# Joining the blocks of the first edge layer, doubling the gather rings, and making the transposed one-hot matrix on ScalarE

## The chip, the cores and the metric

The kernel runs on one core of one Trainium2 chip. The metric is the device time of one execution in microseconds; lower is better. Shares and clocks below are those of the hardware profiler for one profiled execution.

## The reference

Two graph layers follow each other on N = 12,500 nodes with 128 features and E = 212,500 edges (100,000 random edges in both directions and one loop for each node), sorted by destination.

```python
edge_index = jnp.stack([src, dst])
x = _layernorm(x + L0(x, edge_attr_128, WQ, WK, WV, WE, ..., edge_index), axis=-1)
x = _layernorm(x + L1(x, edge_index, W, att_src, att_dst, ..., W1, ..., W2, ...), axis=-1)

# L0: attention over edges, 8 heads of 16
Q, K, V = x @ WQ, x @ WK, x @ WV ;  Eh = edge_attr @ WE
score = K[src] * Q[dst] / sqrt(16) * Eh
score = exp(clip(score.sum(-1), -5, 5))
wV = segment_sum(V[src] * score, dst) ;  Z = segment_sum(score, dst)
h = x + wV / (Z + 1e-6) ;  return batch_norm(h)

# L1: graph attention, softmax over the edges of a destination
xl = x @ W ;  e = leaky_relu((xl @ att_src)[src] + (xl @ att_dst)[dst], 0.2)
alpha = exp(e - segment_max(e, dst)[dst]) / segment_sum(...)
out = segment_sum(alpha * xl[src], dst) + bias
h = bn_relu(out @ W1 + b1) ; h = bn_relu(h @ W2 + b2) ; return h + x
```

All arithmetic is float32.

## The kernel before

Nodes are padded to NP = 12,800 and worked in NG = 25 groups of 512. Edges are worked in NC = 416 chunks of 512, K = 4 slots of 128 edges, one edge per partition. As edges are sorted by destination, the destinations of a chunk nearly always lie in a window of W = 64 nodes that begins at the chunk's first destination (`base_row` holds these bases; the chunks that reach further are worked over again in the `far_windows` functions). Each function is a block of its own: its engines run free of each other, tied by semaphores, and meet at its end.

`prologue` makes the bases and `dst_local`, destination minus base, from the index tables. `project` works the node groups: TensorE transposes x (L341), ScalarE copies it out (L366), TensorE multiplies by the three weight matrices at once (L355), ScalarE evicts Q (L377), VectorE evicts K and V (L391) and copies the transposed x to the third plane of `acc` (L386); SyncE stores `q_table` and `kv_table` in DRAM. `acc` is the accumulator in SBUF, 128 partitions by three planes of 12,800.

`edges0` runs the chunks of the first layer. `U` = 4 is the depth of its rings of data, `V` = 8 that of its index ring and, in layer 1, of its data rings. For each chunk:

- SyncE loads `idx` (L428), the transposed edge features `eat` (L431, 256 KB) and the 64 rows `qw` of `q_table` (L435). These loads, for the chunk four ahead, wait for `spread` of this chunk.
- GpSimd issues four indirect gathers of 128 rows of `kv_table` (L460) into ring slot c mod 4, once TensorE has counted `summed` for the chunk four before.
- VectorE makes `hot` (L548), the 512x64 one-hot matrix, from `dst_local` and `iota`, both in SBUF, three chunks ahead.
- TensorE runs, in this order, the four transposes of `hot` of chunk c+2 into PSUM (`turn`, L479), then for chunk c+1 four matmuls of edge features by WE (L488) and four that spread the Q rows over the edges with the transposed one-hot matrix (L491), which count `spread`, then for chunk c the sums over the window, values (L498) and weights (L500), which count `summed`. The sums wait for VectorE's `valued`.
- ScalarE copies the transposed one-hot matrix out of PSUM for chunk c+2 (L524), then exponentiates the scores of chunk c+1 (L531).
- VectorE multiplies keys by queries (L559), by edge features (L562), reduces over heads (L564), clips (L567), adds the sums of chunk c to `acc` (L581), and weighs the values in place (L573).

`nodes0` divides by the denominators, which go out to DRAM and come back in another layout before they are inverted (L923) and broadcast, adds x on GpSimd (L817), normalizes, and projects for layer 1. `edges1` runs the chunks again with a running maximum: four gathers of 66-float rows on GpSimd (L1064, ring of 8, waiting for `summed`), logits on ScalarE (L1129), mask and maximum on VectorE (L1154 compares with `iota` in SBUF, L1163, L1167), two small transposing products on TensorE (L1081, L1085), `newm` and the shift on VectorE (L1182, L1189), exponentials and the copy of the maximum back to `acc` on ScalarE (L1119 to L1121), then the sums (L1092, L1093) and their addition to `acc` (L1208). `nodes1` finishes.

`alone` is a pass through a semaphore that separates instructions with two waits; `landed` works out the count that a semaphore has when a slot's transfer is in; `over_chunks` runs a body over all chunks in a hardware loop unrolled by its last argument.

Of the kernel before, what the change touches and what calls it, by code (L numbers as in the profile page):

```python
# [21 lines left out]
P = 128  # L22
D = 128
# [10 lines left out]
U, V = 4, 8  # L34
# [12 lines left out]
PIECES = ((0, 3), (3, 12), (12, NG))  # L47
LEAD = 2
# [5 lines left out]
assert V % U == 0 and NG * SG == N and (NG - 5) % 4 == 0 and CR * CJ == NC and LAST % K == 0 and NG % 2 == 1  # L54
# [113 lines left out]
def build(nc, x, src, dst_rows, dst_cols, edges, weights, vectors, out):  # L168
    with ExitStack() as ctx:
# [18 lines left out]
        m["far_table"] = dram("far_table", [NC], I32)  # L188

        m["acc"] = sb("acc", [P, 3, NP])  # L190
# [11 lines left out]
        prologue(nc, m, dst_rows, dst_cols, weights, vectors)  # L202
        project(nc, m, x)
        edges0(nc, m, src, edges)
        far_windows0(nc, m, src, edges)
        nodes0(nc, m)
        edges1(nc, m, src)
        far_windows1(nc, m, src)
# [3 lines left out]
def prologue(nc, m, dst_rows, dst_cols, weights, vectors):  # L212

    with ExitStack() as ctx:
        sem = lambda name: counted(nc, ctx, m, name)
        sb = lambda name, shape, dt=F32: ctx.enter_context(nc.sbuf_tensor(name, shape, dt))
        weights_in, rows_in, cols_in = sem("weights_in"), sem("rows_in"), sem("cols_in")
        base_ready, base_stored, base_back = sem("base_ready"), sem("base_stored"), sem("base_back")
        ident_zero, made, step = sem("ident_zero"), sem("made"), sem("pro_step")

        rows = m["acc"][0:CR, 0, 0:CJ * CE].rearrange("p (j e) -> p j e", e=CE)
        low = m["acc"][0:CR, 1, 0:CJ * CE].rearrange("p (j e) -> p j e", e=CE)
        rows_i = m["acc"][0:CR, 2, 0:CJ * CE].bitcast(I32).rearrange("p (j e) -> p j e", e=CE)
        cols_i = m["acc"][:, 0, CJ * CE:CJ * CE + NC * K].bitcast(I32).rearrange("p (c k) -> p c k", k=K)
# [6 lines left out]
        far_row = sb("far_row", [P, NC + 1])  # L231
        block = ctx.enter_context(nc.Block())

        @block.sync
        def _(sp):
            sp.dma_start(rows_i, dst_rows.rearrange("(p j) e -> p j e", j=CJ)).then_inc(rows_in, 16)
            sp.dma_start(cols_i, dst_cols).then_inc(cols_in, 16)
            sp.wait_ge(base_ready, 1)
            sp.dma_start(m["base_table"].rearrange("(p j) -> p j", j=CJ), base_i[0:CR, :]).then_inc(base_stored, 16)
            sp.dma_start(m["far_table"].rearrange("(p j) -> p j", j=CJ), far_i[0:CR, :]).then_inc(base_stored, 16)  # L240

            sp.wait_ge(base_stored, 32)
# [5 lines left out]
        @block.scalar  # L248
        def _(act):
            act.dma_start(m["w"][:], weights).then_inc(weights_in, 16)  # L250
            act.dma_start(m["vec"][:], vectors).then_inc(weights_in, 16)
            act.wait_ge(weights_in, 32)

        @block.gpsimd
        def _(pool):
# [8 lines left out]
            nc.gpsimd.memset(m["power"][:], -0.5).then_inc(made, 1)  # L264
            pool.wait_ge(made, 4)

        @block.vector
        def _(dve):
# [11 lines left out]
            nc.vector.tensor_copy(far_i[0:CR, :], far_f[0:CR, :]).then_inc(base_ready, 1)  # L280
            dve.wait_ge(cols_in, 16)
            do(nc.vector.tensor_copy(m["dst_local"][:], cols_i))
            dve.wait_ge(base_back, 48)
# [6 lines left out]
            do(nc.vector.tensor_copy(m["base_row"][FAR_ROW:FAR_ROW + 1, NC:NC + 1], reach[:, NC:NC + 1]))  # L290


def project(nc, m, x):

    with ExitStack() as ctx:
        sem = lambda name: counted(nc, ctx, m, name)
        sb = lambda name, shape, dt=F32: ctx.enter_context(nc.sbuf_tensor(name, shape, dt))
        ps = lambda name, shape: ctx.enter_context(nc.psum_tensor(name, shape, F32))
        x_in = [sem(f"x_in{s}") for s in range(4)]
        stored = [sem(f"qkv_stored{s}") for s in range(2)]  # L300
        turned, copied, kept = sem("x_turned"), sem("xt_copied"), sem("xt_kept")
        projected, q_out, kv_out = sem("projected"), sem("q_out"), sem("kv_out")
        xn = sb("xn", [P, 4, T, D])
        xt = sb("xt", [P, 2, G])
        q = sb("q", [P, 2, T, D])
        kv = sb("kv", [P, 2, T, 2 * D])
        ps_xt = ps("ps_xt", [P, 2, G])
        ps_qkv = ps("ps_qkv", [P, T, G])
        xg = x.rearrange("(g k p) d -> g p k d", k=T, p=P)
        qg = m["q_table"].rearrange("(g k p) d -> g p k d", k=T, p=P)  # L310
        kvg = m["kv_table"].rearrange("(g k p) d -> g p k d", k=T, p=P)
        wqkv = m["w"][:, WQ:WV + 1, :].rearrange("p a d -> p (a d)")
        block = ctx.enter_context(nc.Block())

        @block.sync
        def _(sp):
            lead(sp, [*stored], DMA_LEAD)
            for s in range(4):
                sp.dma_start(xn[:, s], xg[s]).then_inc(x_in[s], 16)

            def body(g, s):
                if exists(g + 4):
                    sp.wait_ge(turned, g + 1)
                    sp.dma_start(xn[:, s], row(xg, g + 4)).then_inc(x_in[s], 16)
# [9 lines left out]
        def _(pe):  # L334
            lead(pe, [projected], LEAD)
            def turn_x(g, s):
                pe.wait_ge(x_in[s], landed(g, s, 16, 4))
                if not (isinstance(g, int) and g < 2):
                    pe.wait_ge(kept, g - 1 + LEAD)
# [1286 lines left out]
```

## Time and profile before

| | before |
|---|---|
| runs | 5929.43, 5932.58, 5944.88 us, median 5932.58 |
| profiled execution | 5944.3 us, of it span 5942.5 |
| TensorE busy | 4076.5 us, 69% of the span |
| VectorE busy | 3282.2 us, 55% |
| GpSimd busy | 3368.5 us, 57% |
| ScalarE busy | 1399.3 us, 24% |
| first and last gather of layer 0 | 121.6 and 2886 us |
| first and last gather of layer 1 | 3180.5 and 5706.5 us |

The profile is of one execution; the engine rows give the time in which instructions were recorded as running. A matmul's end is modelled in it. "Idle before" is the time in which an engine stood before an instruction, with what it waited for: "remote" means a semaphore that another engine raised later than the recorded end of its instruction, "issue" that nothing in the profile shows a wait. The granted clock of TensorE is given in shares of full speed.

### The profile page before, as it was taken

What the parts mean: (1) busy time and instruction counts of PE and PEld (TensorE: products, weight loads), DVE (VectorE), ACT (ScalarE), POOL (GpSimd) and SP (SyncE); (2) the same over time, 40 slices, a digit from 0 to 9 for tenths busy, and PEclk for the clock granted to TensorE, in tenths of its full rate; (3) what the DMA queues carried; (4) which work ended last, traced back from release to release, by engine and by line L of the source; (5) the groups of instructions that cost most, each with busy time, mean ns of one, the idle gap of its engine ahead of it and who ended that gap; (6) DMA issues with size and microseconds to landing.
All of it is one profiled execution on the core that took longest, in us unless ns stands there. A gap on an engine that the chain in (4) does not pass through costs nothing. (4 is left out here: it accounts for less than half of the span.)

```text
span 5942.5 us, 93441 instructions
## 1 busy us (share of the span) xinstructions
PE 4076.5 (69%) x21439; PEld 3506.1 (59%) x21440; DVE 3282.2 (55%) x8432; ACT 1399.3 (24%) x4197; POOL 3368.5 (57%) x3417
## 2 busy tenths in 40 slices
PE   5888888888888888888455555555555555555553
PEld 3777787887777777777423444444444444444431
DVE  5554555555555555555474555555555555555555
ACT  2111111111111111111043222222222222222224
POOL 1565555565556555656334666666666666666621
PEclk8787877777778777878676555555555555555566
DMA  7444444444444444444522222222222222222223
GB/s 215 119 126 121 125 123 122 124 125 124 123 123 128 121 123 124 127 121 130 99 58 70 50 51 49 51 50 50 50 51 50 50 51 49 50 51 50 51 69 85
DMA packets 482022, 538.82 MB, mean 91 GB/s; under 512 B 250299, under 2 KB 341053, under 8 KB 481366
## 3 DMA queue, kind: packets, MB, share of 16 engines
q0 software_dynamic: 133120, 330.78, 21.5%
q1 hardware_dynamic: 348199, 203.99, 14.1%
q10 hardware_dynamic: 672, 3.74, 0.5%
q14 instruction: 23, 0.19, 0.0%
q8 instruction: 8, 0.13, 0.0%
HBM read 497.64 MB, written 40.50 MB: 91 GB/s over the span
## 5 line engine op out<-in xcount | busy, mean ns | idle before, releaser
L460 POOL DMA_INDIRECT kv_g<-kv_table,idx x1664 | 1642.8, 987 | 1242.4 <-issue 442.2
L1064 POOL DMA_INDIRECT xg<-xl_table,idx x1664 | 1629.5, 979 | 917.4 <-issue 473.2
L1092 PE MATMUL ps_sum<-pw,xg 128*128 128x64 f32 x3328 | 819.2, 428 | 523.9 <-DVE pws L1194 380.3
L1092 PEld LDWEIGHTS ps_sum<-pw,xg 128*128 128x128 f32 x3328 | 741.0, 328 | 645.9 <-DVE pws L1194 469.4
L498 PE MATMUL ps_sum<-hot,kv_g 128*128 128x64 f32 x3328 | 566.2, 325 | 267.7 <-issue 134.7
L559 DVE TENSOR_TENSOR prod<-ps_q,kv_g 128x512 f32<-128x512 f32 x416 | 286.7, 689 | 803.5 <-remote 526.8
L531 ACT ACTIVATE pex<-score 128x512 f32<-128x512 f32 x416 | 261.6, 629 | 1883.5 <-DVE score L567 1328.6
L498 PEld LDWEIGHTS ps_sum<-hot,kv_g 128*128 128x128 f32 x3328 | 502.4, 231 | 342.9 <-issue 162.2
L488 PE MATMUL ps_eh<-w,eat 128*128 128x128 f32 x3328 | 598.2, 331 | 48.5 <-issue 46.4
L491 PE MATMUL ps_q<-qw,hott 64*128 64x128 f32 x3328 | 578.1, 317 | 42.2 <-issue 40.9
L488 PEld LDWEIGHTS ps_eh<-w,eat 128*128 128x128 f32 x3328 | 548.7, 245 | 70.5 <-issue 64.7
L500 PE MATMUL ps_sum<-hot,pex 128*128 128x64 f32 x3328 | 558.9, 322 | 11.1 <-issue 10.7
L491 PEld LDWEIGHTS ps_q<-qw,hott 64*128 64x128 f32 x3328 | 480.9, 217 | 115.3 <-issue 82.8
L1119 ACT COPY acc<-newm 128x64 f32 x416 | 102.0, 245 | 1831.1 <-remote 1145.0
L500 PEld LDWEIGHTS ps_sum<-hot,pex 128*128 128x128 f32 x3328 | 521.5, 238 | 8.2 <-issue 7.5
L1081 PE MATMUL ps_top<-ident,top 128*64 128x128 f32 x416 | 163.8, 394 | 416.4 <-DVE top L1167 215.0
L1129 ACT ACTIVATE lg<-adw,xg 128x64 f32<-128x64 f32 x1664 | 436.3, 332 | 26.4 <-issue 23.4
L1085 PE MATMUL ps_max<-ident,col 64*128 64x64 f32 x832 | 285.4, 445 | 194.7 <-issue 185.7
L581 DVE TENSOR_TENSOR acc<-acc,ps_sum 128x128 f32 x416 | 120.3, 289 | 475.5 <-PE ps_sum L500 190.2
L479 PE MATMUL ps_hott<-ident,hot 128*64 128x128 f32 x1664 | 323.9, 325 | 60.3 <-DVE hot L548 32.7
L1085 PEld LDWEIGHTS ps_max<-ident,col 64*128 64x128 f32 x832 | 207.5, 309 | 249.4 <-issue 199.8
L1208 DVE TENSOR_TENSOR acc<-acc,ps_sum 128x128 f32 x416 | 117.4, 282 | 428.7 <-remote 406.9
(138 smaller groups left out, 5201.3 us busy)
## 6 DMA issues: line engine op xcount, KB each, us to landing
eat<-in_edges SPq DMA_DIRECT2D x416, 256.0 KB
kv_g<-kv_table,idx POOLq DMA_INDIRECT x1664
xg<-xl_table,idx POOLq DMA_INDIRECT x1664
idx<-in_src SPq DMA_DIRECT2D x832, 2.0 KB
qw<-q_table SPq DMA_DIRECT2D x416, 32.0 KB
adw<-ad_row SPq DMA_DIRECT2D x416, 32.0 KB
kv_table<-kv SPq DMA_DIRECT2D x25, 512.0 KB, 4.1
xl_table<-xl SPq DMA_DIRECT2D x25, 264.0 KB
```

The lines of the kernel that those rows point to most:

```text
L460: nc.gpsimd.indirect_dma_start(out=kv[:, u, k], out_offset=None, in_=m["kv_table"], in_offset=bass.IndirectOffsetOnAxis(ap=idx[:, i, k:k + ...
L479: mm = nc.tensor.transpose(ps_hott[0:W, u % 2, at(k, P)], hot[:, u, k], m["ident"][:])
L488: nc.tensor.matmul(ps_eh[:, b, k], eat[:, u, at(k, P)], m["w"][:, WE], start=True, stop=True)
L491: mm = nc.tensor.matmul(ps_q[:, b, k], hott[:, b, at(k, P)], qw[:, u], start=True, stop=True)
L498: nc.tensor.matmul(ps_sum[:, b, 0:W], kv[:, u, k, D:2 * D], hot[:, u, k], start=(k == 0), stop=(k == K - 1))
L500: mm = nc.tensor.matmul(ps_sum[:, b, W:2 * W], pex[:, b, k], hot[:, u, k], start=(k == 0), stop=(k == K - 1))
L531: nc.scalar.activation(pex[:, b].rearrange("p k (h d) -> p (k h) d", d=DH), score[:, b].unsqueeze(2).to_broadcast([P, K * H, DH]), ACT.Exp ...
L559: nc.vector.tensor_tensor(prod[:].rearrange("p (k d) -> p k d", d=D), ps_q[:, b], kv[:, u, :, 0:D], ALU.mult).then_inc(mult, 1)
L1064: nc.gpsimd.indirect_dma_start(out=xg[:, u, k], out_offset=None, in_=m["xl_table"], in_offset=bass.IndirectOffsetOnAxis(ap=idx[:, u, k:k + ...
L1085: nc.tensor.matmul(ps_max[:, u % 2, 0:W], col[:, u % 2:u % 2 + 1].to_broadcast([W, P]), m["ident"][0:W, 0:W], start=True, stop=True).then_ ...
L1092: nc.tensor.matmul(ps_sum[:, b, 0:W], xg[:, u, k, 0:D], pw[:, b, k], start=(k == 0), stop=(k == K - 1))
L1129: last = nc.scalar.activation(lg[:, u % 4, k], adw[:, u], ACT.Identity, bias=xg[:, u, k, D:D + 1])
```

## The change

The prologue, the projection and the edge stage of layer 0 become one block. x is no longer transposed on TensorE: the host passes `xk`, x transposed with the columns of each group reordered, and `xt`, x transposed. All keys and values are projected first (25 groups of four 128x256 matmuls), evicted by ScalarE alone, and stored in rows of 4 KB, then all queries. GpSimd's gathers start when the keys and values are stored, beside the projection of the queries. Edges of a chunk lie as slot by partition, and the indices of eight chunks are loaded at once.

`acc` has two planes; the third is allocated behind the edge stage and loaded from `xt` in `nodes0`, in the queue behind the store of the denominators and ahead of the load that brings them back. GpSimd's addition of x waits for it.

In the edge stage the ring of gathered rows goes from 4 to 8 in layer 0 and from 8 to 16 in layer 1; the other rings keep depth 4 (layer 0) or 8 (layer 1). TensorE's `turn` is gone, and so is the pass through a semaphore in it. In its place a new DRAM table holds destination minus base for each edge; SyncE loads the chunk's 512 values broadcast over 64 partitions (`local`, 128 KB), and ScalarE makes `hott` = relu(1 - |local - p|) in two steps. `iota` is read from PSUM in the comparisons of both layers. The loops are unrolled twice as far on most engines, one memset moves from VectorE to GpSimd, the last chunk makes one gather instead of four, and in layer 1 the masked logits and `fade` lie in PSUM.

```diff
-U, V = 4, 8
+U, V = 8, 16
+B = 8
+STAGES = 3
-        m["acc"] = sb("acc", [P, 3, NP])
+        m["local_table"] = dram("local_table", [NC, CE])
+
+        m["acc"] = sb("acc", [P, 2, NP])
...
+            def load_local(c, u):
+                sp.dma_start(local[:, u % 4], m["local_table"][bass.ds(c, 1), :].partition_broadcast(W)).then_inc(local_in[u % 4], 16)
...
+            def body(c, v, peeled):
+                sp.wait_ge(spread, c + 1 + LEAD)
+                if not (peeled and c + 4 >= NC):
+                    load_local(c + 4, v)
+                    load_edges(c + 4, v)
+                    load_window(c + 4, v)
+                if v % B == 5 and not (peeled and c + 11 >= NC):
+                    sp.wait_ge(kv_in[7], landed(c, v % U, 16 * K, U))
+                    load_src((c - v) * K + (v // B + 2) * (B * K), v // B)
...
+            for s in range(STAGES):
+                pool.wait_ge(kv_stored[s], 16 * (-(-(NG - s) // STAGES)))
+            for u in range(U):
+                gather(u, u)
...
+            for g in range(NG):
...
+                for k in range(T):
+                    mm = nc.tensor.matmul(ps_pair[:, g % 2, k // 2, at(k % 2, 2 * D)], nodes_x[:, g, k], wkv, start=True, stop=True)
...
+            def copy_out(c, u, first=False):
+                b = u % 2
+                act.wait_ge(local_in[u % 4], landed(c, u % 4, 16, 4))
+                if not first:
+                    act.wait_ge(spread, c - 1 + LEAD)
+                nc.scalar.activation(hott[:, b], local[:, u % 4], ACT.Abs, bias=line[0:W]).then_inc(apart, 1)
+                act.wait_ge(apart, c + 1)
+                nc.scalar.activation(hott[:, b], hott[:, b], ACT.Relu, bias=1.0, scale=-1.0).then_inc(copied, 1)
...
-            def turn(c, u):
-                pe.wait_ge(hot_ready, c + 1)
-                pe.wait_ge(copied, c - 1 + LEAD)
-                alone(pe, m["passed"])
-                for k in range(K):
-                    mm = nc.tensor.transpose(ps_hott[0:W, u % 2, at(k, P)], hot[:, u, k], m["ident"][:])
-                mm.then_inc(turned, 1)
...
-                                        m["iota"][:].unsqueeze(1).to_broadcast([P, K, W]),
+                                        ps_iota.unsqueeze(1).to_broadcast([P, K, W]),
                                         ALU.is_equal).then_inc(hot_ready, 1)
...
             sp.dma_start(m["den_rows"], acc[0:P:DH, 1, :]).then_inc(den_out, 16)
+            for piece, (first, end) in enumerate(PIECES):
+                sp.dma_start(third[:, first * G:end * G], xt[:, first * G:end * G]).then_inc(xt_in[piece], 16)
             sp.wait_ge(den_out, 16)
             sp.dma_start(den[:], m["den_rows"].rearrange("h (a n) -> (h a) n", a=P // H)).then_inc(den_in, 16)
...
-        xg = sb("xg", [P, V, K, ROW1])
-        lg = sb("lg", [P, 4, K, W])
+        raw = sb("raw", [P, 4, K, W])
+        ps_lg = ps("ps_lg", [P, 4, G])
+        lg, fade = ps_lg[:, :, 0:K * W].rearrange("p b (k w) -> p b k w", w=W), ps_lg[:, :, K * W:(K + 1) * W]
```

## Rows read from the trace of the kernel before

**Rows 1.** The page: span, busy time and share of each engine, instructions.

```profile
span 5942.5 us, 93441 instructions
PE 4076.5 (69%) x21439; PEld 3506.1 (59%) x21440; DVE 3282.2 (55%) x8432; ACT 1399.3 (24%) x4197; POOL 3368.5 (57%) x3417
```

**Rows 2.** Stages: length, PE, PEld, DVE, ACT, POOL busy (count), clock, DMA, GB/s.

```profile
0.00:120.00 120.00, 81.04 (x300) 49.26 (x301) 63.48 (x90) 35.44 (x77) 1.14 (x10) 0.99 0.79 239
160.00:2900.00 2740.00, 2343.91 (x14885) 2155.80 (x14884) 1429.26 (x2896) 482.37 (x827) 1626.69 (x1648) 0.79 0.44 123
3224.00:5730.00 2506.00, 1414.32 (x5383) 1174.25 (x5384) 1456.35 (x4539) 685.45 (x2884) 1598.34 (x1632) 0.50 0.26 50
```

**Rows 3.** Groups by line: busy us, mean ns, idle before and its releasers.

```profile
L460 POOL DMA_INDIRECT kv_g<-kv_table,idx x1664 | 1642.8, 987 | 1242.4 <-issue 442.2
L1064 POOL DMA_INDIRECT xg<-xl_table,idx x1664 | 1629.5, 979 | 917.4 <-issue 473.2
L1129 ACT ACTIVATE lg<-adw,xg 128x64 f32<-128x64 f32 x1664 | 436.3, 332 | 26.4 <-issue 23.4
L524 ACT COPY hott<-ps_hott 64x512 f32<-64x512 f32 x151 | 86.6, 573 | 140.2 <-remote 79.2 <-PE ps_hott L479 53.5 <-issue 6.6
```

**Rows 4.** Waits of the whole run: us in total, times, longest.

```profile
DVE prod L559 <- remote: 526.8, 105, 6.9
DVE acc L1208 <- remote: 406.9, 137, 10.0
POOL kv_g L460 <- PE ps_sum L500: 382.6, 201, 17.7
POOL kv_g L460 <- remote: 298.0, 130, 2.8
POOL xg L1064 <- remote: 424.2, 181, 3.1
```

**Rows 5.** Timeline of an undisturbed chunk of layer 0: start, length, idle before.

```profile
1504.99 0.69 DVE L559 TENSOR_TENSOR prod<-ps_q,kv_g 128x512 f32<-128x512 f32 x1 [2.66 <-PE ps_q L491]
1506.63 0.60 PE L479 MATMUL ps_hott<-ident,hot 128*64 128x128 f32 x4
1507.06 1.06 PE L488 MATMUL ps_eh<-w,eat 128*128 128x128 f32 x8
1508.62 1.14 POOL L460 DMA_INDIRECT kv_g<-kv_table,idx  x1 [2.03 <-PE ps_sum L500]
1508.86 0.42 DVE L548 TENSOR_TENSOR hot<-dst_local,iota 128x256 f32<-128x256 f32 x1
1509.34 0.69 DVE L559 TENSOR_TENSOR prod<-ps_q,kv_g 128x512 f32<-128x512 f32 x1
```

**Rows 6.** Timeline of a disturbed stretch of layer 0 and the cold transposes after it.

```profile
1565.90 0.94 POOL L460 DMA_INDIRECT kv_g<-kv_table,idx  x1 [0.30 <-issue]
1568.63 0.69 DVE L559 TENSOR_TENSOR prod<-ps_q,kv_g 128x512 f32<-128x512 f32 x1 [6.67 <-remote]
1569.56 0.94 POOL L460 DMA_INDIRECT kv_g<-kv_table,idx  x1 [2.72 <-remote]
...
1576.15 1.06 PE L479 MATMUL ps_hott<-ident,hot 128*64 128x128 f32 x4
```

**Rows 7.** Timeline: the first gather and the first addition of layer 0.

```profile
121.60 1.15 POOL L460 DMA_INDIRECT kv_g<-kv_table,idx  x1 [119.67 <-DMA idx<-in_src]
...
159.92 0.29 DVE L581 TENSOR_TENSOR acc<-acc,ps_sum 128x128 f32 x1 [1.02 <-issue]
```

**Rows 8.** Timeline: end of layer 1's first eight chunks of gathers.

```profile
3220.22 0.95 POOL L1064 DMA_INDIRECT xg<-xl_table,idx  x1 [0.30 <-issue]
3223.46 0.29 DVE L1208 TENSOR_TENSOR acc<-acc,ps_sum 128x128 f32 x1 [10.00 <-remote]
```

**Rows 9.** Timeline of ScalarE's only table load, and transfers by line with us to landing.

```profile
28.69 1.28 ACT L366 ACT_TABLE_LOAD   x1 [28.56 <-PEq L214]
...
acc<-inv_row SPq DMA_DIRECT2D x1, 3328.0 KB, 17.6
```

More of the change, by code:

```diff
@@ L47 @@
 PIECES = ((0, 3), (3, 12), (12, NG))
+XK_PIECES = ((0, 2), (2, 6), (6, 11), (11, 18), (18, NG))
 LEAD = 2
@@ L264, in _, with gather @@
             nc.gpsimd.memset(m["power"][:], -0.5).then_inc(made, 1)
-            pool.wait_ge(made, 4)
+            nc.gpsimd.iota(line[:], pattern=[[0, 1]], base=0, channel_multiplier=-1,
+                           allow_small_or_imprecise_dtypes=True).then_inc(line_made, 1)
+            pool.wait_ge(line_made, 1)
+            pool.wait_ge(scratch_free, 1)
+            pool.wait_ge(local_stored, 16)
+            nc.gpsimd.memset(acc[:, 0], 0.0).then_inc(clear, 1)
+            def gather(c, v, last=False):
+                u, i = v % U, v // B
+                if u == 0:
+                    pool.wait_ge(src_in[i], landed(c, v, 16, V))
+                alone(pool, m["passed"])
+                for k in range(-(-LAST // P) if last else K):
+                    nc.gpsimd.indirect_dma_start(
+                        out=kv[:, u, k], out_offset=None, in_=m["kv_table"],
+                        in_offset=bass.IndirectOffsetOnAxis(ap=idx[:, i, u * K + k:u * K + k + 1],
+                                                            axis=0)).then_inc(kv_in[u], 16)
@@ L755, in nodes0 @@
         row_out = [sem(f"row_out{s}") for s in range(2)]
-        acc, vec, w = m["acc"], m["vec"], m["w"]
+        acc, third, vec, w = m["acc"], m["third"], m["vec"], m["w"]
+        xt_in = [sem(f"xt_in{piece}") for piece in range(len(PIECES))]
         stats = sb("bn_slices", [P, NG, 6])
@@ L814, in _ @@
         def _(pool):
-            with pool.Fori(0, NG) as g:
-                pool.wait_ge(divided, g + 1)
-                nc.gpsimd.tensor_tensor(acc[:, 0, at(g, G)], acc[:, 0, at(g, G)], acc[:, 2, at(g, G)],
-                                        ALU.add).then_inc(h_ready, 1)
+            for piece, (first, end) in enumerate(PIECES):
+                pool.wait_ge(xt_in[piece], 16)
+                with pool.Fori(first, end) as g:
+                    pool.wait_ge(divided, g + 1)
+                    nc.gpsimd.tensor_tensor(acc[:, 0, at(g, G)], acc[:, 0, at(g, G)], third[:, at(g, G)],
+                                            ALU.add).then_inc(h_ready, 1)
             pool.wait_ge(bn_var, 1)
@@ L957, in add_x @@
                 dve.wait_ge(hn_ready, g + 1)
-                nc.vector.tensor_tensor(y[:, s], hn[:, s], acc[:, 2, at(g, G)], ALU.add).then_inc(y_ready, 1)
+                nc.vector.tensor_tensor(y[:, s], hn[:, s], third[:, at(g, G)], ALU.add).then_inc(y_ready, 1)
             def node_moments(g, s):
@@ L1321, in body @@
                 nc.scalar.activation(fade[:], drop[:], ACT.Exp)
-                nc.scalar.copy(acc[:, 2, bass.ds(base, W)], newm[:])
+                nc.scalar.copy(third[:, bass.ds(base, W)], newm[:])
                 nc.scalar.activation(pw[:], lg[:], ACT.Exp).then_inc(weighed, 1)
```

549 lines of the change are left out of this document (247 added, 302 removed).

## The prediction

> **What bounds the kernel now.** I read the page first, then the stages, then who waits for whom, then the timeline of single chunks. No engine fills the span: TensorE is the busiest with 69% [rows 1]. The two edge stages hold 5246 of 5942 us [rows 2]. GpSimd's count in them, at four gathers a chunk, gives the pace: 1648 gathers are 412 chunks in 2740 us, 6.65 us a chunk in layer 0; 1632 are 408 chunks in 2506 us, 6.14 us in layer 1. TensorE's clock is granted at 0.79 on average in layer 0 and at 0.50, the 1.2 GHz level, in layer 1, where the engine is busy 56% of the time [rows 2].
>
> Against these paces stand two floors. A gather takes 0.987 us in layer 0 and 0.979 in layer 1 [rows 3], and 0.30 us lie between gathers where GpSimd waits for nothing [rows 6, 8]: four are 5.15 and 5.12 us. An undisturbed chunk of layer 0 goes round in 1509.34 - 1504.99 = 4.35 us, with VectorE and TensorE both without a gap [rows 5]. So the pace lies above both floors, and the question is what is late. It isn't the gathered rows: ScalarE's logits, which are the first to need them in layer 1, stand idle for only 26.4 us in all [rows 3], and GpSimd itself waits on TensorE's sums (382.6 and 298.0 us in layer 0, 424.2 in layer 1) because its ring is full [rows 4]. What is late are results of TensorE that arrive well behind the recorded end: VectorE waits 526.8 us on "remote" at its first multiplication in layer 0 and 406.9 us at its last addition in layer 1 [rows 4]. The disturbed stretch shows the pattern: gathers run back to back, VectorE stands 6.67 us for a product, and within a microsecond of its release GpSimd starts again after 2.72 us of standstill [rows 6]. At the start of layer 1 the same addition waits 10.00 us and is released 2.3 us after the last gather of the fill [rows 8]. I take from this that a cycle is a run of gathers with TensorE's results late, plus a restart of some two microseconds. Why they are late the trace doesn't settle. The ring of 8 in layer 1 waits on "remote" as often and as long at GpSimd (181 times, 424.2 us, a mean of 2.3) as the ring of 4 in layer 0 (130 times, 298.0 us, also 2.3) [rows 4].
>
> **The change part by part.**
>
> *Start to the first addition.* The first gather is issued at 121.60 and the first addition made at 159.92 [rows 7]. The first 120 us move data at 239 GB/s [rows 2], 28.7 MB. What must move ahead of the first gather is afterwards x (6.6 MB), the keys and values (13.1), and about 2 of indices and weights; the 6.6 MB of Q move later. 21.7 MB at that rate are 91 us, so the gathers start 31 us earlier. But the fill is eight chunks (8 x 5.0 = 40 us) instead of four, and if TensorE's results are held back during it, as in layer 1 [rows 8], the first addition comes at about 91 + 40 + 9 = 140. The Q projection lies beside the fill. I take -20 us; bounds -45 (the fill costs nothing) and +15 (the Q stores and GpSimd's memset hold up the fill).
>
> *The transposes.* Four transposes go, and with them their wait for `hot`. The next matmul starts 0.43 us behind them at full clock [rows 5], and they last 1.06 us at the low one [rows 6]. Where VectorE sets the undisturbed chunk (4.35 us without a gap), nothing is gained. Bounds 0 and 1.06 us a chunk; I take 0.25, some half of the warm price, because the restarts are bound by TensorE and the rest is not: 416 x 0.25 = 104 us.
>
> *The two ScalarE steps.* The copy of 0.573 us [rows 3] becomes two steps over the same 64x512, which I price at 0.573 each; the second waits for the first. ScalarE is busy 482 us in 2740 [rows 2], 1.17 us a chunk, and comes to 1.75 of 6.65. They are made two chunks ahead and no longer wait for TensorE. Queued behind them is the exponential of the next chunk, for which VectorE's value step waits. Nothing is lost while the pair ends before the scores do; if the exponential always met the second step, it would cost 0.57 a chunk. I take 0, bounds 0 and +238.
>
> *The load of `local`* adds 128 KB to the 512 KB or so that a chunk moves. The DMA engines are busy 0.44 of layer 0 [rows 2], so this goes to about 0.5 and is hidden; it stands in SyncE's queue ahead of the loads of `eat` and `qw`, four chunks ahead. One load of indices per eight chunks replaces eight small ones. Together 0, bounds -10 and +30.
>
> *`iota` in PSUM.* Gathers that nothing disturbs last 0.94 us [rows 6, 8], against the mean of 0.987. The one of 1.14 us runs beside the comparison that reads both inputs from SBUF [rows 5]. Where these vanish, a chunk of gathers is 4 x 0.04 = 0.16 us shorter, and as GpSimd's run is a part of the cycle I count it whole in layer 0, -67 us, and half in layer 1, -30; bounds 0 and -130 together.
> The Trainium skill ("SBUF — State Buffer", Who interferes with whom) says of this that a VectorE instruction with two SBUF inputs contends with GpSimd's reads, but infers that `tensor_tensor` doesn't stall descriptor generation. By that inference the gather of 1.14 us would have another cause and the sum would lack these 97 us, while the row speaks for the contention.
>
> *The deeper rings.* In the steady state I count them at nothing: GpSimd's ring is full before and would be full after, so a slot more moves no wait away. At the ends they cost: behind the first addition layer 0 has four chunks fewer to gather at 6.65 us and four more to drain at 4.35, -9 us. In layer 1 the fill of eight more at 5.12 and the drain at 4.35, in place of eight at 6.14, are +27. The last chunk's three gathers less are -8 in both layers together.
>
> *The third plane.* 6.55 MB of `xt` stand in SyncE's queue behind the store of the denominators and ahead of the load that brings them back. A load of 3328 KB into `acc` lands after 17.6 us [rows 9], so 6400 KB take 34. The load of denominators, the inverse and its broadcast all come behind. I take +28, bounds 0 (queues that serve both at once) and +40.
>
> The sum: -20 - 104 + 0 + 0 - 97 - 9 + 27 - 8 + 28 = -183 us. The profiled execution took 5944.3 us, so 5761; the median of the runs shown is 11.7 us lower, and the forecast goes by it: 5750 us. With the bounds of the terms of size, this mechanism alone spans about 5640 to 5930.
>
> **The rivals.**
>
> *A. The deeper rings set GpSimd free.* If the results are late because GpSimd stops and starts at a full ring, and not because of its runs, a ring twice as deep lets it run through. Both layers then go at the gather floor, 5.0 us a chunk: 412 x 1.65 + 408 x 1.14 = 1145 us less, about 4820; with the mean gather as it is, 5.15, 1018 less, about 4950. If only layer 0 gets there, some 5300. For it speaks that the floors of the other engines lie lower still; against it, that layer 1 has a ring of 8 already and gains only half a microsecond, with work that differs.
>
> *B. The longer runs hold TensorE's results back for longer, and the kernel gets slower.* The place is the first multiplication in layer 0 and the last addition in layer 1, together 934 us on "remote" [rows 4]. It decides from the point at which these waits grow by 183 / 934 = 20%. The longest wait grows from 6.9 to 10.0 us, by 45%, from the ring of 4 to that of 8 [rows 4]; by that the cost is 420 and the time 5750 + 420 = 6170; by half of it 5960, and for the case as a whole I name 6010. For it speaks the release 2.3 us after the fill's last gather; against it, the equal mean waits of GpSimd in both layers.
>
> *C. Nothing that matters changes*: VectorE and GpSimd set the cycle, the transposes were hidden, and the ends cancel out. Then -20 - 9 + 27 - 8 + 28 = +18 us stand against half of the term for `iota`, -48: 5932.6 - 30, about 5900, and with no gain from `iota` 5950.
>
> *D. ScalarE reloads its table* for each of Abs, Relu and Exp. One load takes 1.28 us [rows 9]. Two a chunk on the way to the exponential are 416 x 2.56 = 1065 us at most; half of it hidden, the time is 5750 + 530 = 6280. Against it: Exp, Identity and the copies share one load in the kernel before, and only Abs is new.
> The Trainium skill ("ScalarE: Activation LUTs", Table sets: the hidden batching unit) has abs, relu and copy in every set, by which D doesn't happen; that the trace shows a single load agrees with it for all but Abs.
>
> **How the numbers follow.** Chances: the forecast's mechanism 0.54, A 0.12, B 0.20, C 0.12, D 0.02. The predicted time is that of the first, 5750. For the range I leave out A with 0.12 and the far end of B and D with 0.07, and go beyond the mechanism's own 5640 downwards, as layer 0 could reach its floor in part: 5450 to 6050. What this kernel's runs can tell from no change is about 0.3%, 18 us. Faster by more: 0.54 less 0.02, A, and 0.05 of C, 0.69; within: 0.09; slower: B, D and the rest of C, less what B leaves within, 0.22.
>
> **What would show each step.** In the profile after: first gather near 91 us and first addition near 140; layer 0 at 6.25 us a chunk and layer 1 at 6.05, from the count of gathers; gathers of 0.95 us on average; no idle of VectorE on ScalarE's exponential; a single table load; "remote" waits about as they were; and some 28 us more between the last addition of layer 0 and the first division. The prediction is wrong if GpSimd's waits on the sums vanish (A), if the remote waits grow by a fifth (B), or if VectorE comes to wait on ScalarE.

## The result and the profile after

The changed kernel takes 6398.18 us (median of four runs, 6396.37 to 6403.21), the kernel before 5931.01 beside it: a ratio of 1.0787, with a 95% interval of 1.0765 to 1.0809. The profiled execution has a span of 6397.3 us, 454.8 more than before. It was forecast 180 us faster; it is 467 us slower.

The page of the changed kernel, its head and the clock's row of the 40 slices:

```profile
span 6397.3 us, 87512 instructions
PE 4800.7 (75%) x19875; PEld 4254.5 (67%) x19876; DVE 3149.3 (49%) x8359; ACT 1685.2 (26%) x4613; POOL 3312.5 (52%) x3413
PEclk8555555555555555555559555555555555555556
```

Beside [rows 1], TensorE has 1564 instructions less and is busy 724 us more. The row of the clock says why: in layer 0, from the second slice to the twenty-first, it is granted at 0.5, which is the 1.2 GHz level, where it was at 0.79 on average [rows 2].

The middle of layer 0 in the table by stretches of the changed kernel (length, then TensorE, weight loads, VectorE, ScalarE, GpSimd busy with counts, clock, DMA share, GB/s):

```profile
1000.00:2000.00 1000.00, 1000.00 (x4314) 939.44 (x4314) 467.00 (x943) 251.38 (x404) 526.38 (x540) 0.50 0.45 128
```

TensorE is busy for all of 1000 us and everybody else has time to spare. 540 gathers are 135 chunks, 7.41 us a chunk, against 6.65 [rows 2]. A round of the timeline (start, length, engine, line, idle time before):

```profile
1000.48 2.07 PE L410 MATMUL ps_pair<-qw,hott 64*128 64x128 f32 x8
...
1002.48 1.97 PE L418 MATMUL ps_sum<-hot,kv_g 128*128 128x64 f32 x8
1002.59 0.69 DVE L525 TENSOR_TENSOR prod<-ps_pair,kv_g 128x512 f32<-128x512 f32 x1 [2.50 <-PE ps_pair L410]
...
1004.24 1.91 PE L420 MATMUL ps_sum<-hot,pex 128*128 128x64 f32 x8
...
1005.95 2.02 PE L406 MATMUL ps_pair<-w,eat 128*128 128x128 f32 x8
```

Four groups of eight passes, none with idle time before it, each 1.9 to 2.1 us long, where the same eight passes of the edge matmuls took 1.06 [rows 5]. VectorE now waits for TensorE at its first multiplication in 411 of 416 chunks (2.50 us here), and by the waits of the whole run GpSimd does too:

```profile
POOL kv_g L361 <- PE ps_sum L420: 1055.2, 390, 42.8
DVE prod L525 <- PE ps_pair L410: 1032.3, 411, 2.8
DVE acc L547 <- PE ps_sum L420: 535.6, 398, 3.9
POOL xg L1038 <- remote: 345.7, 116, 11.7
POOL xg L1038 <- DMA idx<-in_src_cols: 110.4, 23, 20.0
```

What [rows 4] showed in layer 0, results that came late by "remote", is gone: no engine has such a wait in layer 0 any more. By stages (boundaries are the first and last gathers and additions of the timeline):

| stage | before | after | difference |
|---|---|---|---|
| start to first gather | 121.6 | 78.4 | -43.2 |
| first gather to first addition | 38.3 | 82.1 | +43.8 |
| first to last addition, layer 0 | 2745.8 | 3076.6 | +330.8 |
| to the first gather of layer 1 | 274.8 | 289.2 | +14.4 |
| layer 1 to its last addition | 2550.3 | 2659.4 | +109.1 |
| the rest | 211.7 | 211.6 | 0 |

Layer 0 holds three quarters of the loss, layer 1 most of the rest.

### The profile page after: what moved, and what is told of

Its sections match the earlier page's. It is cut to its first block and busy times, and to the rows that moved or that the text cites. A ratio compares the mean times of both kernels' runs of the same rounds, so it can differ in the third digit from the quotient of the medians.

```text
span 6397.3 us, 87512 instructions
## 1 busy us (share of the span) xinstructions
PE 4800.7 (75%) x19875; PEld 4254.5 (67%) x19876; DVE 3149.3 (49%) x8359; ACT 1685.2 (26%) x4613; POOL 3312.5 (52%) x3413
## 5 line engine op out<-in xcount | busy, mean ns | idle before, releaser
L410 PE MATMUL ps_pair<-qw,hott 64*128 64x128 f32 x3328 | 862.4, 438 | 3.6 <-DMA qw<-q_table 3.6
L406 PE MATMUL ps_pair<-w,eat 128*128 128x128 f32 x3328 | 840.6, 434 | 4.1 <-issue 4.1
L418 PE MATMUL ps_sum<-hot,kv_g 128*128 128x64 f32 x3328 | 818.1, 427 | 2.7 <-DVE kv_g L539 2.7
L410 PEld LDWEIGHTS ps_pair<-qw,hott 64*128 64x128 f32 x3328 | 740.1, 325 | 97.1 <-issue 93.2
L418 PEld LDWEIGHTS ps_sum<-hot,kv_g 128*128 128x128 f32 x3328 | 740.0, 327 | 95.9 <-issue 95.9
L525 DVE TENSOR_TENSOR prod<-ps_pair,kv_g 128x512 f32<-128x512 f32 x416 | 287.7, 692 | 1039.9 <-PE ps_pair L410 1032.3
L406 PEld LDWEIGHTS ps_pair<-w,eat 128*128 128x128 f32 x3328 | 759.5, 333 | 4.5 <-issue 4.5
L420 PEld LDWEIGHTS ps_sum<-hot,pex 128*128 128x128 f32 x3328 | 759.7, 333 | 0.0
L1060 PE MATMUL ps_tops<-ident,col 64*128 64x64 f32 x832 | 285.4, 445 | 318.2 <-issue 303.1
L1105 ACT ACTIVATE raw<-adw,xg 128x64 f32<-128x64 f32 x1664 | 437.4, 336 | 26.1 <-DMA xg<-xl_table,idx 26.1
```

The source lines that it names most:

```text
L406: nc.tensor.matmul(ps_eh[:, b, k], eat[:, u % 4, at(k, P)], m["w"][:, WE], start=True, stop=True)
L410: mm = nc.tensor.matmul(ps_q[:, b, k], hott[:, b, at(k, P)], qw[:, u % 4], start=True, stop=True)
L418: nc.tensor.matmul(ps_sum[:, b, 0:W], kv[:, u, k, D:2 * D], hot[:, u % 4, k], start=(k == 0), stop=(k == K - 1))
L420: mm = nc.tensor.matmul(ps_sum[:, b, W:2 * W], pex[:, b, k], hot[:, u % 4, k], start=(k == 0), stop=(k == K - 1))
L525: nc.vector.tensor_tensor(prod[:].rearrange("p (k d) -> p k d", d=D), ps_q[:, b], kv[:, u, :, 0:D], ALU.mult).then_inc(mult, 1)
L1060: nc.tensor.matmul(ps_max[:, u % 2, 0:W], col[:, u % 2:u % 2 + 1].to_broadcast([W, P]), m["ident"][0:W, 0:W], start=True, stop=True).then_ ...
```

## The experiments

The experiments ran on several chips, and these are of two kinds for this program: the unchanged kernel before takes 5931 and 6018 us on two occasions, and 4958, 4977, 4955 and 4961 on four others. So every time below stands beside that of the kernel before on the same chip. Below, a slow chip is one of the first kind and a quick chip one of the second. Each chip was met on one occasion only, so whether the chip or the occasion makes the kind isn't shown, and no profile of the unchanged kernel before was taken on a quick one. The clock of layer 0 is read from the table by stretches, 1000 to 2000 us.

**Is it the clock, and do the transposes lift it?** The first kernel puts four transposes back as idle work:

```diff
+            def turn_idle(c, u):
+                pe.wait_ge(hot_ready, c + 1)
+                alone(pe, m["passed"])
+                for k in range(4):
+                    nc.tensor.transpose(ps_idle[0:W, at(k, P)], hot[:, u % 4, k], m["ident"][:])
             def body(c, u, peeled):
+                turn_idle(c, u)
```

> The changed kernel with four transposes of the one-hot matrix put back ahead of each chunk's edge matmuls in layer 0; nobody reads what they write, so they are pure extra work for TensorE. In the changed kernel TensorE has no idle time in layer 0, its clock is granted at 0.50 throughout and a chunk takes 7.42 us. Theory (clock): the transposes were what lifted the clock. Then the granted clock of layer 0 goes back to about 0.8 and the chunk to between 5.2 and 6.6 us, so the whole takes 5500 to 6070 us in spite of the extra work. Rival (work): the clock has another cause (rings, order of edges, the joined block); then it stays at 0.50 and four transposes add 0.85 us to each chunk, 8.27 us, the whole 6750 us.

It took 4858.14 us beside 4957.69 of the kernel before, a ratio of 0.9801 (0.9772 to 0.9829). The changed kernel itself stands at 1.1811 on another quick chip (g1_after below), and on this one it took 5832.69 us with a single other edit (e2_ring4 below). Twelve per cent more instructions for TensorE in layer 0, and the layer is a third shorter. Its clock around the start and in the middle of layer 0, from the table by stretches of e1_turns:

```profile
130.00:140.00 10.00, 7.45 (x32) 6.67 (x32) 9.09 (x8) 1.87 (x3) 0.00 (x0) 0.50 0.19 57
140.00:150.00 10.00, 10.00 (x63) 9.43 (x63) 5.17 (x11) 2.80 (x5) 4.51 (x5) 0.72 0.38 108
150.00:160.00 10.00, 9.75 (x81) 9.11 (x81) 8.09 (x17) 4.69 (x8) 7.73 (x8) 1.00 0.67 204
1000.00:2000.00 1000.00, 917.95 (x7024) 860.05 (x7023) 678.64 (x1363) 364.64 (x585) 762.68 (x780) 0.93 0.65 185
```

And the same for the changed kernel at its start:

```profile
150.00:160.00 10.00, 8.50 (x38) 7.79 (x37) 8.17 (x11) 2.76 (x5) 0.00 (x0) 0.50 0.31 92
160.00:170.00 10.00, 10.00 (x44) 9.33 (x44) 4.69 (x10) 2.85 (x5) 5.11 (x6) 0.50 0.37 98
170.00:180.00 10.00, 10.00 (x46) 9.33 (x44) 4.46 (x9) 1.87 (x3) 5.87 (x7) 0.50 0.40 121
```

Both begin the layer at the low level. With the transposes TensorE works without a gap and the clock rises; without them it works just as gaplessly, and the clock stays. The kernel before climbs in the same way, again and again. Here are the microseconds ahead of [rows 5] and behind them, from its table by stretches:

```profile
1496.00:1500.00 4.00, 4.00 (x20) 3.78 (x19) 2.25 (x4) 0.20 (x1) 1.89 (x2) 0.50 0.50 156
1500.00:1504.00 4.00, 4.00 (x19) 3.67 (x19) 1.23 (x3) 1.00 (x2) 1.88 (x2) 0.50 0.17 41
1504.00:1521.00 17.00, 14.38 (x111) 12.58 (x110) 7.69 (x16) 2.30 (x4) 9.84 (x11) 1.00 0.43 122
1521.00:1531.00 10.00, 8.00 (x38) 7.37 (x37) 6.17 (x13) 2.31 (x4) 5.17 (x5) 0.50 0.47 125
```

It works gaplessly at 0.50 and the clock rises; then TensorE stands idle for part of the time (14.38 of 17 us busy), and the clock falls.

In e1_turns, with the clock up, 780 gathers are 195 chunks in 1000 us, 5.13 us a chunk: GpSimd's floor of 5.0 to 5.15, and the next bound. The time lay below the expected 5500 to 6070, which was made for the chip of the result; this one was a quick one.

**The ring.**

```diff
             for u in range(U):
+                if u >= 4:
+                    pool.wait_ge(summed, u - 3 + LEAD)
                 gather(u, u)
-                pool.wait_ge(summed, c + 1 + LEAD)
+                pool.wait_ge(summed, c + 5 + LEAD)
```

> The changed kernel with GpSimd's gathers in layer 0 held back so that only four slots of the ring of eight are in use. Theory (clock): the ring has no part in it, the chunk stays at 7.42 us, the clock at 0.50, the whole within 20 us of 6398. Rival (rings): the deeper ring has made TensorE's work so even that it never bursts; with four slots the clock comes back in part and the whole falls to 5950 to 6200 us.

5832.69 us beside 4957.69; layer 0 took 3077 us between its additions, to the microsecond what it takes with eight slots. The ring has no part in it.

**Fewer transposes in the kernel before.** e3_before1 leaves one of four from the third chunk on, h4_before0 none; h4_before0 also takes out ScalarE's wait for them. The pass through a semaphore in front of the transposes stays in both, so this isn't what holds the clock up. Most of the transposed one-hot matrix is stale in both.

```diff
-                for k in range(K):
+                for k in range(K if isinstance(c, int) and c < 2 else 1):    # e3_before1; 0 in h4_before0
                     mm = nc.tensor.transpose(ps_hott[0:W, u % 2, at(k, P)], hot[:, u, k], m["ident"][:])
```

> The kernel before with one transpose per chunk instead of four (from the third chunk on), so that three quarters of the transposed one-hot matrix are stale and the output of layer 0 is not the reference's. Nothing else of its work changes. Theory (clock): with the transposes mostly gone the granted clock of layer 0 falls from 0.79 towards 0.50 and the kernel gets slower with less work: 6.9 to 7.6 us a chunk, 6050 to 6350 us. Rival (work): the clock stays near 0.79 and the kernel gets faster, by up to 0.33 us a chunk, 5800 to 5930 us.

5013.99 us beside 4957.69: slower with less work, but by 1.1% only, in one execution.

```profile
1000.00:2000.00 1000.00, 937.27 (x6150) 873.18 (x6149) 646.83 (x1306) 209.63 (x374) 745.75 (x750) 0.81 0.54 153
```

The expected range was for the other kind of chip. Over the whole execution the granted clock is 0.672, against 0.704 to 0.707 for the kernel before beside it, so it fell less than the theory said. One transpose is enough to keep most of the clock.

> The kernel before with no transposes from the third chunk of layer 0 on; ScalarE's copy stays, of stale data, so the output of layer 0 is not the reference's. Theory (clock): it goes the way of the changed kernel, layer 0 at a granted clock of 0.50 and 7.4 us a chunk, the whole 850 to 950 us over the kernel before on a chip without late results, 300 to 400 us over it on one with them. Rival (something else of the joined block holds the clock down): the clock of layer 0 stays near 0.8 and the time within 100 us of the kernel before.

5893.52 us beside 4954.65, 939 us over the kernel before. Its stretch and the round of its timeline:

```profile
1000.00:2000.00 1000.00, 1000.00 (x4314) 939.48 (x4313) 468.39 (x945) 148.13 (x270) 517.96 (x539) 0.50 0.40 111
```

```profile
1500.95 2.02 PE L489 MATMUL ps_eh<-w,eat 128*128 128x128 f32 x8
1502.90 2.07 PE L492 MATMUL ps_q<-qw,hott 64*128 64x128 f32 x8
1504.91 1.97 PE L499 MATMUL ps_sum<-hot,kv_g 128*128 128x64 f32 x8
1506.66 1.91 PE L501 MATMUL ps_sum<-hot,pex 128*128 128x64 f32 x8
```

This is the changed kernel's layer 0, in count (4314 passes), clock and round, with none of the change's other parts: 3076 us between the additions, against 3077. Taking the transposes away from the kernel before, with the one wait for them, is enough to bring layer 0 to this length, and the changed kernel has it on either kind of chip. So the missing transposes make the whole of the loss of layer 0. How large the loss is depends on what it is compared with. On the quick chips the changed kernel is 903 us behind the kernel before (g1_after), on the chip of the result 467, as the kernel before is itself slowed there.

**How much, and of what kind?**

```diff
-                for k in range(4):
+                for k in range(1):                                    # f2_one
-                for k in range(4):
+                for k in range(2):                                    # f3_matmul
-                    nc.tensor.transpose(ps_idle[0:W, at(k, P)], hot[:, u % 4, k], m["ident"][:])
+                    nc.tensor.matmul(ps_idle[0:W, at(k, P)], hot[:, u % 4, k], m["ident"][:], start=True, stop=True)
-                turn_idle(c, u)
+                if u == 0:                                            # f4_eighth
+                    turn_idle(c, u)
```

> The kernel before, unchanged, for its profile where it takes 4958 us and not 5931. Theory: the thousand microseconds between the two are the late results of TensorE; this profile has no waits on remote, and both layers go at GpSimd's gather floor of 5.1 to 5.2 us a chunk, with TensorE's clock near 0.8 in layer 0. Rival: the waits are there as before, only shorter.

This chip was a slow one: 6014.35 us, and the profile is much like the recorded one (remote 516.2 us at L559, 487.7 at L1208). So this run couldn't tell what the late results cost, but it is the base of its three neighbours.

> The changed kernel with one idle transpose per chunk of layer 0 instead of none or four. Theory (clock, a matter of how much TensorE does): one transpose is 0.1 us of work and is not enough for a chunk without idle time at 0.50 to lift the clock; the whole stays near 5834 us or, as it adds 0.2 us a chunk, 5900. Rival (a matter of kind: any transpose lifts it): the clock goes to 0.9 and the whole to 4860 us.

> The changed kernel with two ordinary idle matmuls (four passes, the same operands and widths) instead of four transposes. Theory (amount): the passes are as many as those of the four transposes, so the clock is lifted in the same way and the whole is 4860 us within 20. Rival (kind): only transposes do it, the clock stays at 0.50 and the whole is about 5834 + 0.85 x 416 = 6190 us.

> The changed kernel with four idle transposes in every eighth chunk only. Theory (two stable states): once lifted, the clock stays up as long as TensorE keeps its pace, and a push in every eighth chunk is enough to get there; the whole comes to 4860 us within 40. Rival (dose): what counts is the work of each stretch, and seven chunks of eight without it fall back; the clock stays below 0.65 and the whole above 5500 us.

The middle of layer 0 for f1_before, f2_one, f3_matmul and f4_eighth, in this order:

```profile
1000.00:2000.00 1000.00, 858.00 (x5371) 787.05 (x5371) 517.29 (x1050) 174.24 (x299) 588.46 (x599) 0.78 0.43 123
```

```profile
1000.00:2000.00 1000.00, 876.80 (x4752) 811.53 (x4752) 500.57 (x1012) 269.49 (x432) 567.70 (x578) 0.67 0.47 137
```

```profile
1000.00:2000.00 1000.00, 911.55 (x5058) 808.10 (x5059) 485.78 (x983) 261.98 (x420) 554.20 (x563) 0.72 0.46 134
```

```profile
1000.00:2000.00 1000.00, 922.82 (x4598) 861.08 (x4598) 489.00 (x991) 264.36 (x424) 552.64 (x566) 0.61 0.46 135
```

In the table, a low stretch is a time at 0.50 in the trace's record of the granted clock that begins and ends within layer 0.

| | whole | to before beside it | clock, layer 0 | layer 0 | low stretches, mean us |
|---|---|---|---|---|---|
| changed kernel (recorded) | 6398 | 1.079 | 0.50 | 3077 | never rises |
| four transposes in each eighth chunk | 6292 | 1.045 | 0.61 | 2935 | 39 of 54.7 |
| two ordinary matmuls a chunk | 6306 | 1.048 | 0.72 | 2943 | 84 of 19.5 |
| one transpose a chunk | 6204 | 1.031 | 0.67 | 2841 | 96 of 18.7 |
| kernel before (f1_before) | 6014 | 1.00 | 0.78 | 2775 | 110 of 10.9 |

Every dose lifts the clock in part and shortens the layer. So it isn't a matter of kind, ordinary matmuls do it too; and not of two stable states either, since a push in each eighth chunk gives 0.61, neither 0.50 nor 0.93. One transpose did more than the theory allowed.

The last column says where the doses act. Every fall comes behind idle time of TensorE (105 falls in layer 0 of the recorded kernel before), and nearly every rise straight out of gapless work, in these runs as above. What the dose changes most is how long a low stretch lasts: 54.7 us with four transposes in each eighth chunk, 18.7 with one a chunk, 10.9 in the kernel before, and on a quick chip 14.5 with one (e3_before1) and 4.9 with four idle ones (e1_turns). Why gapless work without any of them never ends a low stretch stays open.

These four runs are of one execution each on a slow chip, where late results add idle time of their own; between runs of one kernel (e1_turns, g2_turns, h1_turns, i1_turns) layer 0 differs by 9 us.

**The four transposes beside the changed kernel, on one chip.**

> The changed kernel, unchanged, beside the next three. Theory: layer 0 at 0.50 and 7.42 us a chunk on any chip; on a chip where the kernel before takes 4960 us the whole is 5834 us, on one where it takes 5930 to 6020 it is 6400 us.

> The changed kernel with four idle transposes per chunk of layer 0, as e1_turns. Theory: the clock is up and the whole is faster than the changed kernel on either chip. On a chip that runs the kernel before in 5930 to 6020 us, results of TensorE come late once the clock is up, and the chunk goes to 6.2 to 6.9 us: 5900 to 6200 us; on one that runs it in 4960 us, 4860 us. Rival: where results are late the transposes bring nothing, and it stays at 6400 us.

> As g2_turns, with the gathers of layer 0 held back to a ring of four. It prices the deeper ring once the clock is up. Theory: the ring is full or the gathers are the bound either way, so the two are within 20 us. Rival: the deeper ring saves the waits on the sums that the kernel before shows, and four slots cost over 50 us.

| quick chip, before 4976.83 | whole | ratio (95%) | layer 0 | layer 1 |
|---|---|---|---|---|
| g1_after | 5879.86 | 1.1811 (1.1777 to 1.1846) | 3077 | 2159 |
| g2_turns | 4911.80 | 0.9867 (0.9838 to 0.9895) | 2101 | 2162 |
| g3_turns4 | 4924.42 | 0.9892 (0.9863 to 0.9921) | 2126 | 2162 |

The repair takes 968 us off. The deeper ring is worth 12.6 us once the clock is up, which is within what two runs each can tell of the whole, though layer 0 itself is 25 us longer with four slots. Four executions of the repaired kernel give its place against the kernel before:

> The changed kernel with four idle transposes per chunk of layer 0, as g2_turns, timed in three rounds against the kernel before. On a chip without late results: 0.987 of the kernel before, within 0.005. On a chip with them the theory (clock) gives 5900 to 6200 us, 0.98 to 1.03 of the kernel before; the rival (transposes bring nothing there) 1.08.

4858.76 beside 4954.65, ratio 0.9805 (0.9789 to 0.9822), just outside the expected 0.987 within 0.005. i1_turns is the same kernel once more, again on a quick chip: 4870.58 beside 4960.91. What the repair is worth on a slow one stays open.

> The changed kernel with four idle transposes per chunk of layer 0. On a chip with late results the theory (clock) gives 5900 to 6200 us, 0.98 to 1.03 of the kernel before, where the changed kernel had 1.079. On a chip without them 0.98.

**Layer 1: the indices, and an idle TensorE.** The load of eight chunks' indices is put at the head of the eight instead of in their middle:

```diff
+                if u % B == 0 and not (peeled and c + 16 >= NC):
+                    sp.wait_ge(xl_in[u + 7], landed(c, u, 16 * K, V) + past[u + 7])
+                    load_src((c - u) * K + (u // B + 2) * (B * K), u // B)
                 sp.wait_ge(largest, c + 1)
...
-                if u % B == 4 and not (peeled and c + 12 >= NC):
```

> The changed kernel with the load of the next eight chunks' indices in layer 1 issued four chunks earlier, ahead of the window's load. In the changed kernel GpSimd waits 110.4 us in 23 waits for this load, 20.0 of it at the first. Theory: that is where layer 1 lost its time against the kernel before (6.30 against 6.08 us a chunk in the middle); the waits go to about 20 us and the whole to 6398 - 90 = 6308 us. Rival: the waits move elsewhere, as TensorE's results are late anyway, and the whole stays within 20 us of 6398.

> As h1_turns, with layer 1's indices loaded four chunks earlier (the edit of e4_idx). On a chip with late results: the theory says that GpSimd's 23 waits for the indices cost layer 1 90 us, so it is 90 us less than h1_turns; the rival that they lie beside late results anyway and nothing changes. On a chip without late results: no change, within 15 us.

> As i1_turns, with layer 1's indices loaded four chunks earlier. On a chip with late results 90 us less than i1_turns if the waits for indices cost layer 1 its time, the same if not. On a chip without them the same within 15 us.

5836.33 us without the transposes (e2_ring4, with the old place, took 5832.69), and with them 4866.39 beside 4858.76 and 4864.67 beside 4870.58: nothing, on chips where GpSimd waits for these indices only once, 20.1 us at the first. On the chips with late results it waits 23 to 25 times, 110.4 us in the recorded run and 135.8 in f2_one, but all these runs met quick ones, so the edit wasn't tried where it could matter.

```diff
+                for k in range(8):
+                    nc.tensor.matmul(ps_idle[:, 0:P], m["ident"][:], m["w"][:, WK], start=True, stop=True)
             over_chunks(pe, body, NC, V)
```

> As g2_turns, and in layer 1 eight idle 128x128 matmuls per chunk behind the sums into a free PSUM bank (for which the comparison of layer 1 reads iota from SBUF again). Theory (idle TensorE): where results are late in layer 1, they are so because TensorE stands idle beside the gathers; kept busy it has no remote waits and layer 1 falls from 6.3 to 5.2 us a chunk on such a chip, 450 us less than g2_turns. Rival: the lateness has nothing to do with idle time; the remote waits of layer 1 stay above 700 us and the time is that of g2_turns or longer.

> As g4_fill: h1_turns with eight idle matmuls per chunk in layer 1. On a chip with late results the theory (idle TensorE) says layer 1 falls by 450 us, the rival that it doesn't fall. On a chip without them: no change within 20 us, with the clock of layer 1 at 0.86 and not 0.50, since the gathers are the bound.

Idle matmuls in layer 1 lift its clock from 0.50 to 0.86, as this stretch of g4_fill shows, and gain nothing in the time: 4904.92 beside 4911.80, and 4870.80 beside 4858.76.

```profile
4000.00:4500.00 500.00, 425.29 (x2810) 387.31 (x2808) 321.45 (x1067) 168.29 (x679) 381.75 (x388) 0.86 0.28 59
```

388 gathers are 97 chunks in 500 us, 5.15 a chunk: layer 1 is at the gathers' floor, where TensorE's clock is worth nothing. Whether late results come of an idle TensorE couldn't be seen there.

## Why the prediction was wrong

The step that failed is *the transposes*, and before it the reading of what bounds the kernel. It priced four transposes at 0 to 1.06 us a chunk of TensorE's time and took the granted clock of layer 0, 0.79, as given. Removing them took the clock with it. At the low level the other 32 passes take 7.42 us a chunk, so the term of -104 us is a loss: layer 0 as a whole (-104, -67 for `iota`, -9 for the ring) was forecast 180 us shorter and is 331 longer. h4_before0 shows that this edit alone brings layer 0 to 3076 us. None of the four rivals had it: B put the slowing in late results of TensorE, and these vanish in layer 0 of the changed kernel.

The reading before it failed at [rows 5]. The prediction has VectorE and TensorE both without a gap in the round of 4.35 us and lets VectorE set it. But VectorE stands idle in that round, for the sums of TensorE:

```profile
1508.05 0.29 DVE L581 TENSOR_TENSOR acc<-acc,ps_sum 128x128 f32 x1 [0.70 <-PE ps_sum L500]
```

From 1505.00 to 1509.30 TensorE is busy for 4.30 us and VectorE for 3.47. TensorE alone has no gap, so the round follows its clock.

The rows had the warning. The round at the full clock is 4.35 us, 0.43 of it transposes [rows 5], and four transposes that last 0.60 us there [rows 5] last 1.06 at the low level [rows 6]. So the other 32 passes, 3.92 us, come to twice that at most at 1.2 GHz, 7.84 (7.42 as measured), and with the transposes to over 8: above the pace of 6.65. So layer 0 lived on the higher clock in a way that layer 1, at 0.50 and 56% busy, didn't, and a rival "the clock isn't lifted any more" could have been written with its price, 416 x (7.84 - 6.65) = 495 us at most; by the measured 7.42 it is 320. What the rows couldn't give is whether it would happen.
The Trainium skill ("TensorE: Matmul & The Clock Gate", What's actually happening) says that activity releases the throttle and that the gate goes by how busy the engine has been. The trace doesn't agree, if busy is read as in the profile: 1000.00 of 1000 us busy, 0.50.

The other steps:

- *Start.* The gathers start at 78.4 us (forecast 91) and the first addition comes at 160.5, not 140. The fill cost more than forecast there; on the quick chips the first addition came at 140 to 144 with the ring of eight.
- *The ScalarE steps* cost nothing on the path, as forecast. They take 0.706 and 0.630 us, not 0.573, and VectorE's value step waits for the exponential queued behind them once, 0.7 us, as in the kernel before. The table is loaded once, 1283 ns; rival D did not occur.
- *`iota` in PSUM.* That a gather takes longer beside a VectorE instruction with both inputs in SBUF holds. In layer 0 of the changed kernel all 408 gathers that begin beside the value step take 1.06 us on average, the others 0.95. A longer one from e1_turns:

```profile
1501.69 0.68 DVE L547 TENSOR_TENSOR kv_g<-kv_g,pex 128x512 f32<-128x512 f32 x1
1501.82 1.38 POOL L362 DMA_INDIRECT kv_g<-kv_table,idx  x1 [0.30 <-issue]
```

  But the gather of 1.14 us in [rows 5] begins 0.24 us ahead of the comparison, beside the value step, and that step stayed as it was. A gain by `iota` isn't shown in layer 0: the mean gather went from 987 to 975 ns, and h4_before0, at the changed kernel's pace and with `iota` in SBUF, has 962 where g1_after has 973. In layer 1 the mean went from 979 to 955, but hardly by `iota`. On the chip of h1_turns (955 ns, layer 1 of 2114 us), h3_fill reads `iota` from SBUF again, beside its idle matmuls, and has 961 ns and 2122 us; on another chip g1_after to g3_turns4 have 982 to 984 with `iota` in PSUM, and g4_fill 984 with it in SBUF. So the term of -97 us was worth some 8 us at most in layer 1.
  What layer 1 did gain is seen in h4_before0 beside h1_turns, on one chip: 986 against 955 ns, 2169 against 2114 us. In h4_before0, 180 gathers that begin beside the mask (L1165, both inputs in SBUF) last over 1.1 us; in h1_turns, where the masked logits lie in PSUM, none of the 223 that begin beside it does. The prediction had no term for that move. No run tests it alone.
- *The deeper rings* are neutral in layer 0 at the low clock, as forecast (e2_ring4), and worth some 25 us of it with the clock up (g3_turns4).
- *The third plane* cost 14.4 us (forecast 28; bounds 0 and 40).
- *Layer 1* was forecast within a few us of before and is 109 us longer on the chip of the result, and again in f2_one to f4_eighth (2694 to 2700 us against 2589 of f1_before). The 23 waits for indices hold 90 us of it beyond the first. That they are the cause isn't shown: the edit that moves the load had no effect on quick chips, and wasn't tried on a slow one.
- *Rival A*, GpSimd set free at 5.0 to 5.15 us a chunk, is what every quick chip shows once the clock is up, and it isn't the ring that does it: g3_turns4, with four slots in layer 0, makes 778 gathers in 1000 us, 5.14 us a chunk, and e3_before1, with the rings of the kernel before, goes at 5.33 in layer 0 and 5.15 in layer 1.

## What to carry to other kernels

Price a stage at both levels of TensorE's clock before taking work off the engine. If its pace lies between the two prices, the stage lives on the higher level, and removing matmuls can cost far more than they take: here 0.43 us of transposes a chunk held up 2.3 us (7.42 against 5.06). If the clock doesn't rise in a stage where TensorE never stands idle, a few idle transposes into a free bank are a repair worth one run: here they took 968 us off the changed kernel, and left it 1 to 2% ahead of the kernel before, on quick chips.

## What the runs showed of the hardware

- A TensorE that is busy in every microsecond of a stage of 3 ms, by the modelled ends of the profile, with fp32 matmuls of 64 and 128 columns in a gapless row, can stay at the 1.2 GHz level throughout; four transposes more in each chunk of 32 passes bring it to a granted 0.92 to 0.93 on quick chips. Layer 0 without them took 3076 or 3077 us on four chips, of either kind.
- The same program took 20% longer on two chips than on four others (the kernel before 5931 and 6018 against 4955 to 4977 us), each met on one occasion, with gathers of much the same mean (955 to 987 ns against 954 to 996). What differs in the profiles are the waits on results of TensorE behind their recorded end, up to 15.2 us long in the recorded profile of the kernel before (ScalarE at L1119) and 10.0 at VectorE; there are none in any profile on the quick chips, and none on the slow chip of the result in the layer where TensorE never stands idle. Neither the cause nor a cure was found.
- A faster clock isn't worth anything by itself: from 0.50 to 0.86 in layer 1, and no gain, as GpSimd's four gathers of 0.98 us, with 0.30 us between them, set the pace.
